# A transformer layer of 32 batches: the steady lists of four engines and the bank table in a new order

## The reference

```python
h = _layernorm(x, axis=-1) * (1 + ca) + sa
x = x + ga * attention(h)      # rmsnorm, q k v, softmax(causal(q k^T / 8)) v, sigmoid gates, Wout
h = _layernorm(x, axis=-1) * (1 + cb) + sb
x = x + gb * ffn(h)            # silu(h Wg + bg) * (h Wu + bu) Wd + bd, plus the experts
# experts: sim of h with 2 x 64 keys in each of 4 heads, top 8 of each, top 8 of the sums,
# softmax over those, and sum of silu(h . down[e]) * weight * up[e]
```

## Time and profile before

| what | value |
|---|---|
| median of 3 runs | 1404.91 us |
| lowest, highest | 1401.65, 1404.97 us |
| the profiled execution | 1400.69 us |
| its span, first to last instruction | 1398.8 us |
| PE busy | 1369.1 us |
| PEld busy | 1157.3 us |
| DVE busy | 1214.9 us |
| ACT busy | 1264.6 us |
| POOL busy | 1080.4 us |
| granted TensorE clock | 1.000 |

### The profile page before, as it was taken

The page is one execution under the profiler, slowest core; times in us unless marked ns, Lnnn a source line. Parts: engine busy times, 40 slices in busy tenths (PEclk is TensorE's granted clock), DMA queues, the critical chain, the costliest instruction groups (busy, mean ns, idle before and its releaser), DMA issues.

```text
span 1398.8 us, 39734 instructions
## 1 busy us (share of the span) xinstructions
PE 1369.1 (98%) x11491; PEld 1157.3 (83%) x11491; DVE 1214.9 (87%) x5314; ACT 1264.6 (90%) x4212; POOL 1080.4 (77%) x1252
## 2 busy tenths in 40 slices
PE   6899999999999999999999999999999999999998
PEld 4778888888888888888888888888888888888877
DVE  6688898988898988898988898988898988898877
ACT  6889999999999999999999999999999999999975
POOL 2158888888888888888888888888888888888770
DMA  4000000000000000000000000000000000000000
GB/s 137 16 19 19 17 10 20 21 21 17 15 9 21 21 21 17 15 9 21 21 21 17 15 9 21 21 21 17 15 9 21 21 21 17 15 9 24 11 15 11
DMA packets 51042, 27.74 MB, mean 20 GB/s; under 512 B 10337, under 2 KB 50209, under 8 KB 51009
## 3 DMA queue, kind: packets, MB, share of 16 engines
q1 hardware_dynamic: 50768, 26.91, 7.3%
q10 hardware_dynamic: 240, 0.43, 0.1%
HBM read 23.02 MB, written 4.31 MB: 20 GB/s over the span
## 4 chain that ended last, share of the span: by engine, by line
PE 93%; DVE 3%; ACT 2%; issue 1%; POOL 1%; DMA 0%; SPq 0%; DVEq 0%; POOLq 0%
PE pW L1580 12%; PE pS L1648 12%; PE pW L1582 10%; PE pW L1581 10%; PE pW L1661 9%; PE pW L1689 8%; PE pS L1638 8%; PE pS L1634 7%; PE pW L1731 4%; PE pW L1734 4%; PE pW L1665 4%; PE pW L1722 2%; PE pW L1594 2%; ACT pS L693 1%; DVE pS L1126 0%
## 5 line engine op out<-in xcount | busy, mean ns | idle before, releaser
L693 ACT ACTIVATE pS<-pS,nmx 128x128 f32<-128x128 f32 (+1 forms) x1024 | 390.0, 437 | 31.3 <-DVE nmx L1126 30.7
L525 POOL TENSOR_TENSOR fexp<-fexp,fsum 128x512 f32<-128x512 f32 x240 | 316.5, 1347 | 90.6 <-DVE fexp L1277 90.6
L1126 DVE CUSTOM_DVE_ANT_0 pS<-pS,mask 128x128 f32<-128x128 f32 (+1 forms) x1024 | 332.3, 387 | 51.4 <-PE pS L1638 49.4
L516 POOL TENSOR_TENSOR fsum<-ex 128x512 f32<-128x512 f32 x248 | 251.8, 1047 | 1.3 <-ACT ex L741 1.3
L685 ACT COPY pT<-pS 128x768 f32<-128x768 f32 x256 | 206.1, 817 | 24.1 <-PE pS L1648 23.8
L1648 PE MATMUL pS<-ident,p_sb 128*128 128x128 f32 x1536 | 206.7, 274 | 6.8 <-DVE p_sb L1151 6.6
L1151 DVE TENSOR_TENSOR p_sb<-pS,coef 128x256 f32<-128x256 f32 (+2 forms) x512 | 208.9, 449 | 4.5
L693 ACT ACTIVATION_READ_ACCUMULATOR pS<-pS,nmx 128x1 f32 x1024 | 198.4, 194 | 0.0
L1648 PEld LDWEIGHTS pS<-ident,p_sb 128*128 128x128 f32 x1536 | 175.2, 141 | 27.6 <-DVE p_sb L1151 8.5
L1661 PE MATMUL pW<-pT,v 128*64 128x256 f32 x1024 | 162.3, 395 | 0.1
L1277 DVE TENSOR_SCALAR fexp<-fsum,top,rz 128x512 f32<-128x512 f32 x240 | 156.3, 702 | 0.0
(11 more groups left out here) (211 smaller groups left out, 3674.0 us busy)
## 6 DMA issues: line engine op xcount, KB each, us to landing
x_in<-in_L_attn_tokens SPq DMA_DIRECT2D x32, 128.0 KB, 2.1
x_res<-in_L_attn_tokens SPq DMA_DIRECT2D x32, 128.0 KB, 2.8
modB<-mods_dram SPq DMA_DIRECT2D x32, 128.0 KB, 2.9
modA<-mods_dram SPq DMA_DIRECT2D x31, 128.0 KB, 3.1
out<-yo SPq DMA_DIRECT2D x31, 128.0 KB, 1.9
modC<-mods_dram SPq DMA_DIRECT2D x32, 64.0 KB, 3.1
fsum<-in_L_attn_Wkv SPq DMA_DIRECT2D x1, 512.0 KB, 6.4
w_out<-in_L_attn_Wout SPq DMA_DIRECT2D x1, 512.0 KB, 7.3
```

What stands on the lines that cost most here:

```text
L516: ins = nc.gpsimd.tensor_tensor(fsum[:, k, h], ex[:, k, h, 0:NX].unsqueeze(2).broadcast_to([P, NX, NK]), ex[:, k, RH + h, :].unsqueeze(1). ...
L525: ins = nc.gpsimd.tensor_tensor(fexp[:, k, h, :], fexp[:, k, h, :], fsum[:, k, h].rearrange("p i j -> p (i j)"), ALU.mult)
L693: ins = nc.scalar.activation(ps, ps, ACT.Exp, bias=nmx[:, p % 2, h, k:k + 1], scale=-1.0, accum_out=den(p)[:, h, k:k + 1])
L1126: ins = nc.vector.tensor_tensor_reduce(out=ps, in0=ps, in1=mask[:, (1 - k) * P:2 * P], scale=-1.0, scalar=LARGEST, op0=ALU.add, op1=ALU.mi ...
```

## The change

The steady list of each of PE, ACT, DVE and POOL is written in another order, and the bank table with it. Every operation stays as it was, with the same shapes and waits on the same results; bodies -1, 0 and 32 keep their lists.

```diff
-        order = [("GU", 1, -2), ("D", 0, -2), ("V", 0, 0), ("PV", 6, -1), ("PV", 7, -1), ("V", 3, 0), ("QK", 2, 0),
...
+        order = [("V", 1, 0), ("V", 3, 0), ("V", 0, 0), ("PV", 6, -1), ("PV", 7, -1), ("QK", 2, 0), ("QK", 3, 0),
+                 ("D", 0, -2), ("QK", 4, 0), ("V", 4, 0), ("GU", 1, -2), ("op", 0, -1), ("GU", 2, -2), ("GU", 3, -2),
...
@@ POOL
                 products(0)
                 candidates()
+                add_bias()
                 products(1)
-                rstd1()
-                add_bias()
                 weigh(0)
                 add_heads(0)
+                rstd1()
                 fold(0)
@@ ACT, the head of the period
-                gate_up(1)
-                down_tanh(0)
+                values(1)
                 copy_transposes(7, -1)
                 values(0)
+                values(3)
...
                 copy_transposes(0, 0)
                 copy_transposes(1, 0)
-                queries(5)
-                values(5)
-                gate_up(2)
+                down_tanh(0)
+                gate_up(1)
+                queries(4)
+                values(4)
                 exp_scores(2)
@@ DVE, the head of the period
                 ln1(stats1)
-                bias_product(1)
-                ln1(aggregate1)
-                gate_product(1)
                 sum_top()
-                gated_down(0)
+                invert_top()
+                choose(0, 0)
                 row_max(0)
-                invert_top()
                 row_max(1)
-                ln1(center1)
-                choose(0, 0)
+                invert(0)
                 choose(0, 1)
...
+                choose(1, 0)
+                gated_down(0)
                 row_max(2)
                 row_max(3)
...
                 bias_product(3)
                 gate_product(3)
+                ln1(center1)
+                ln1(scale1)
+                ln1(shift1)
+                ln1(square1)
                 choose(1, 1)
@@ PE, the middle of the period
                 transpose_scores(3, 0)
+                project_qk(5)
+                transpose_experts(0)
+                project_down(1)
+                transpose_h()
+                project_qk(6)
+                project_qk(7)
                 scores(4)
+                scores(5)
                 weigh_values(2)
-                transpose_h()
-                scores(5)
                 weigh_values(3)
-                project_qk(7)
-                transpose_experts(0)
                 project_v(2)
@@ PE, the end of the period
+                project_ffn(1)
                 gate_up(0)
-                project_ffn(1)
-                transpose_scores(6, 0)
                 project_qk(0)
                 project_qk(1)
+                transpose_scores(6, 0)
```

More of the change, by code:

```diff
@@ L904, in body @@
                     return
-                gate_up(1)
-                down_tanh(0)
+                values(1)
                 copy_transposes(7, -1)
                 values(0)
+                values(3)
                 exp_scores(0)
                 weighted(6)
-                values(3)
                 weighted(7)
+                exp_scores(1)
                 queries(2)
-                values(4)
-                exp_scores(1)
+                scale_head(1)
                 queries(3)
-                queries(4)
-                down_tanh(1)
-                scale_head(1)
                 copy_transposes(0, 0)
                 copy_transposes(1, 0)
-                queries(5)
-                values(5)
-                gate_up(2)
+                down_tanh(0)
+                gate_up(1)
+                queries(4)
+                values(4)
                 exp_scores(2)
@@ L929, in body @@
                 total(0)
-                values(1)
+                gate_up(2)
                 gate_up(3)
                 scale_head(3)
-                queries(6)
                 copy_transposes(2, 0)
                 weighted(0)
+                weighted(1)
                 rows2()
+                queries(5)
+                experts(0)
+                down_tanh(1)
+                modulate_h()
                 copy_transposes(3, 0)
-                weighted(1)
+                high_part(h2T_high, h2T, "hT")
+                queries(6)
+                queries(7)
                 exp_scores(4)
-                modulate_h()
                 weighted(2)
-                high_part(h2T_high, h2T, "hT")
+                exp_scores(5)
                 weighted(3)
-                exp_scores(5)
-                queries(7)
                 scale_head(5)
                 copy_transposes(4, 0)
-                experts(0)
                 values(2)
+                values(5)
                 copy_transposes(5, 0)
+                expert_exp(0)
                 rms_scale()
                 weighted(4)
-                expert_exp(0)
                 total(1)
+                exp_scores(6)
+                high_part(xT_high, xT, "xT")
+                expert_exp(1)
                 weighted(5)
-                exp_scores(6)
-                expert_exp(1)
-                high_part(xT_high, xT, "xT")
                 experts(1)
                 exp_scores(7)
+                gate_up(0)
                 scale_head(7)
-                gate_up(0)
+                queries(0)
                 copy_transposes(6, 0)
-                queries(0)
                 queries(1)
@@ L1465, in body @@
                 ln1(stats1)
-                bias_product(1)
-                ln1(aggregate1)
-                gate_product(1)
                 sum_top()
-                gated_down(0)
+                invert_top()
+                choose(0, 0)
                 row_max(0)
-                invert_top()
                 row_max(1)
-                ln1(center1)
-                choose(0, 0)
+                invert(0)
                 choose(0, 1)
-                invert(0)
-                ln1(scale1)
                 coefficients(0)
+                normalise(0)
                 invert(1)
-                normalise(0)
                 coefficients(1)
                 normalise(1)
-                ln1(shift1)
-                gated_down(1)
                 choose(1, 0)
+                gated_down(0)
                 row_max(2)
@@ L1489, in body @@
                 invert(2)
+                ln1(aggregate1)
+                bias_product(1)
                 coefficients(2)
+                gate_product(1)
                 normalise(2)
-                bias_product(2)
+                gate_attention()
                 invert(3)
-                gate_product(2)
-                gate_attention()
                 add_residual()
-                coefficients(3)
                 stats2()
                 aggregate2()
-                ln1(square1)
+                coefficients(3)
                 normalise(3)
+                bias_product(2)
+                gate_product(2)
                 bias_product(3)
                 gate_product(3)
+                ln1(center1)
+                ln1(scale1)
+                ln1(shift1)
+                ln1(square1)
                 choose(1, 1)
+                gated_down(1)
+                low_part(h2T_high, h2T, "hT")
                 row_max(4)
@@ L1507, in body @@
                 invert(4)
-                low_part(h2T_high, h2T, "hT")
                 coefficients(4)
@@ L1514, in body @@
                 row_largest(0)
+                shift(0)
                 row_largest(1)
-                shift(0)
+                shift(1)
                 row_max(6)
-                shift(1)
+                row_max(7)
+                low_part(xT_high, xT, "xT")
                 invert(6)
                 coefficients(6)
-                row_max(7)
                 normalise(6)
+                gate_output()
                 invert(7)
+                finish()
                 coefficients(7)
-                low_part(xT_high, xT, "xT")
-                gate_output()
-                finish()
+                normalise(7)
                 bias_product(0)
                 gate_product(0)
-                normalise(7)
                 if first:
@@ L1913, in body @@
                     return
-                gate_up(1)
-                project_down(0)
                 transpose_scores(7, -1)
+                project_v(1)
+                project_v(3)
                 project_v(0)
@@ L1923, in body @@
                 weigh_values(7)
-                project_v(3)
                 project_qk(2)
+                project_qk(3)
+                project_down(0)
+                project_qk(4)
                 project_v(4)
[L1927 to L1932, removed]
                 transpose_scores(0, 0)
                 transpose_scores(1, 0)
-                project_v(1)
+                gate_up(1)
                 scores(2)
@@ L1938, in body @@
                 project_out()
-                project_qk(6)
+                gate_up(2)
                 gate_up(3)
@@ L1944, in body @@
```

(10 more changed lines are left out.)

## The result

The changed kernel takes 1425.31 us, the median of 4 runs (1419.12 to 1427.11), against 1404.94 for the kernel before beside it (1401.65 to 1405.91): ratio 1.014 [1.012, 1.016], so 20 us slower where 11 us faster was forecast. The profiled execution took 1424.71 us.

The account below looks back on a forecast made before the run. PE, issuing without a pause, was taken to bound the kernel: 0.85 us saved per period less 0.55 given back, net 0.30 made 0.35, times 30 periods is 10.5 us, so 1400.69 becomes 1390 (1394 in median terms); range 1379 to 1407.

Parts of the forecast that it names:

- The saving on PE: Four terms on PE's list together save 0.80 to 0.90 us per period, taken as 0.85.
- The floor of 41.12: PE's period in us with 0.85 saved, before any stalls from the other engines.
- Grouping: On PE, two score groups then two value groups, instead of alternating, save 0.34 us per period.
- h: Transposes of h on PE, moved behind plain full-array work, take 0.19 us instead of 0.36: 0.17 less.
- the two waits: PE's waits at GU3 (DVE product) and QK0 (low part of x) go: 0.16 and 0.13 us less.
- the price of one change: Cost of one change of array shape on PE: 0.11 us each, from 0.34 for three.
- the head, pairs 0 and 1: DVE masks beside POOL's products delay row_max(0), so PE's transposes T1 start at 9.5 instead of 9.13: stall 0.35 us.
- I count 0: PE blocks QK5, V4 and V5, waiting for banks with 0 to 0.2 us of room, were given no stall.
- The small waits: Stalls on PE of 0.15 us for pairs 4 and 5 and 0.05 at the output projection.
- C: Rival: late square1 delays POOL's chain to products(0), choose(0,0) waits; period 42.4, 12 us slower, 1417; 13 in 100.
- B: Rival: new waits of 0.75 to 0.95 us eat the saving, change within 4 us, about 1404; 17 in 100.
- The forecast's own test: Forecast is wrong if PE shows over 0.9 us of waits per period, or under 0.2.

Follow-up runs that it names:

- the last experiment: Transposes of h moved behind the second of two value groups on PE, bank table and ACT's list to match, against the two-waits version: 1408.86 us.
- old-order run: Kernel before with invert_top and the mask call choose(0,0) moved directly ahead of row_max(0) on DVE: 1443.64 us, ratio 1.027.
- two-waits version: Kernel before with bias_product(2) and gate_product(2) ahead of normalise(2), and low_part of x ahead of invert(7), on DVE: 1395.56 us, ratio 0.993.

## Why the prediction was wrong, point by point

**The saving on PE was right.** The floor of 41.12 is found again at about 41.1. Grouping was 0.34 and is 0.36 in PE's blocks, though taking it away costs this period only 0.13; h was 0.17 and measures 0.17 in the last experiment; the two waits were 0.29 and bring 0.26 to 0.27 of the period when taken away alone. What was off is the price of one change: S, W, S, W has two changes more than S, S, W, W, not three, so one costs 0.18; with h between them three changes went, for 0.34 and 0.17 together, 0.17 each. The prediction divided the 0.34 by three and called it 0.11. The sum did not hang on it.

**The step that failed is the head, pairs 0 and 1: stall 0.35, with "I count 0" for V4 behind the copy of QK2.** Its mechanism, masks beside POOL's products ahead of row_max(0), was there. Three sizes were off:

- The start. The masks were to start at 1.3 and take 2.32, with row_max(0) at 3.6. S0 stands at 2.03 in those terms (696.63), so the masks started at 1.62, took 2.48, and row_max(0) came at 4.02: 0.9 late instead of 0.5.
- The reserve. I let the lateness count only at T1, behind 0.15 us of slack. The old-order run shows 1.04 of lateness costing 1.35 in a list with 2.4 us more room to T0. What decides is when ACT frees the banks behind exp_scores(0) and exp_scores(1) in its list, not the next use of the scores.
- The pass. "They stand on engines that moved with PE" was the faulty reason for 0: ACT did not move with PE, it stood idle 1.50 for row_max(0) and came late to the copy of QK2. That makes 1.1 at the head in place of 0.35. The prediction had said that with the pair at 1.0 the stall would be nothing; with the products cut down it is 0.23.

The contention rule of the Trainium skill ("GPSIMD Engine Reference", section 1. Specifications) spoke against this change, as the prediction said, and by the runs it is what makes it slower: 0.92 of 1.5 us of stalls go with POOL's second products. The trace agrees that the two engines slow each other; which of the page's two conditions the masks meet, no run shows. The weight given to it was wrong.

**The small waits** were forecast at 0.2 (0.15 for pairs 4 and 5, 0.05 at the output projection) and are some 0.4, at more places, with none at the output projection; I did not separate them by a run of their own. That T1 would be the place was wrong in the changed kernel, and right only once V4's wait was taken away.

**The rivals.** C had the sign, and not the mechanism. Its step, products(0) late for choose(0,0), is refuted: POOL ended products(0) at 693.6, 2.6 us before the masks, and though rms1 waits 2.7 us for ms, as C wanted, POOL still waits 2.7 for masks later on. B's amount, 0.75 to 0.95 of waits, was passed. The forecast's own test held: over 0.9 us of waits per period means it is wrong. The failure lay in the range: I added stalls as if each were met by a PE free to be late, and gave no chance to one stall passing through two lists at full size.

**What the periods leave.** 28 of them at +0.65 are 18 of the 24 us between the spans. The rest is in bodies outside the steady state: some 2.5 us in the first steady ones, and about 3 in the head of the program, whose lists are the same. There the granted clock was lower, in the changed kernel and, in part, in a faster one (the last section); that the clock is the whole of the 3 is not shown.

## What to carry to other kernels

An operation set ahead of a score chain costs its length as it will be beside whatever the other engine runs at that time, and the lateness must be followed along every list, queue by queue, to the first buffer it frees, not to the next use of the same result. A reserve of 2 us on the tensor engine's side is none if a first-in, first-out engine between holds the bank's release behind the late work. Take each small wait away by itself before a regrouping: here two moves of a few calls gave 0.27 us a period, and the regrouping with them lost 0.65.

## What the runs showed of the hardware

**DVE beside POOL.** A pair of masks takes 0.97 to 1.00 us with POOL idle, and 2.32 beside POOL's weighing, 2.48 beside its products; the product group slows too, 4.05 to 4.43. One mask takes 1.26 to 1.30 there and 0.51 to 0.54 in the pair at 701.20. A row maximum under the end of the same products is not stretched: 0.28 at 698.62, against 0.30 in the earlier trace rows.

**The granted clock at the head.** The kernels have the same lists there, and the clock was at its lower level in one of them. Changed kernel, then the kernel before, over two short stretches:

```profile
22.00:25.00 3.00, 0.94 (x8) 0.73 (x8) 2.69 (x12) 3.00 (x10) 0.00 (x0) 1.00 0.01 5
25.00:28.00 3.00, 3.00 (x16) 2.02 (x16) 1.99 (x10) 0.28 (x1) 2.10 (x4) 0.50 0.17 38
```

```profile
22.00:25.00 3.00, 1.38 (x14) 1.05 (x13) 2.82 (x13) 2.71 (x6) 0.00 (x0) 1.00 0.01 3
25.00:28.00 3.00, 2.82 (x28) 1.75 (x26) 1.55 (x9) 1.87 (x8) 2.67 (x4) 1.00 0.19 44
```

The lower level, 1.2 GHz, follows three microseconds in which PE was busy for 0.94; in the kernel before it was busy for 1.38 and the clock stayed at 2.4. The two-waits version had 0.89 and 0.77 in later stretches of the same head (28 to 35 and 35 to 39 us) and is faster all the same. This belongs to the single execution at least as much as to the kernel: with the masks behind the row maxima PE was busy for 1.37 and 2.82 in the two stretches, as in the kernel before, and the clock was 0.86 and 0.50 later (28 to 35 and 35 to 39), and over 17 runs of the kernel before the mean clock went from 0.994 to 0.999 and the time from 1403.26 to 1408.99.

The last block that stands in all heads alike (L1575) starts at 55.87 us in the changed kernel, at 53.71 in the two-waits version and at 52.41 in the kernel before; 0.6 of the 3.5 was there at 22.4, before the clock fell. The first output projection starts at 68.76, 67.04 and 65.74. So the head is worth up to 3 us, and since its lists are the same I take it for no effect of the steady lists; no run of its own shows it.
